# Moving the statistics of a token tile ahead of the apply before it, and one copy from VectorE to ScalarE, in the first loop of an 8-core attention and slot-router layer

## The chip, the cores and the metric

The kernel runs on all 8 cores of one Trainium2 chip, the same program on each, with no exchange between them. The metric is the device time of the slowest core, in microseconds (us), and the median over runs. A core has five engines that work side by side: PE (TensorE, matmuls and transposes), ACT (ScalarE, functions of one input), DVE (VectorE, elementwise work and reductions), POOL (GpSimd) and SP (SyncE); the last two here only issue transfers. Each runs its own instructions in program order and meets the others through semaphores.

## The reference

The input is x of shape (2, 8192, 1024). One layer is `x + s * silu(f)`, with s an attention block with MLP on the normalised x, and f a slot router on the same normalised x. The part that the change touches is the router's first half, which every core computes for all 8192 tokens of its batch entry (16 tiles of 512), since it sums over them:

```python
xn = (x - mean(x)) / sqrt(var(x) + 1e-5)              # per token, over 1024
h = gelu(concat([xn, slot_mean]) @ w1 + b1)           # 512 wide
route_logits = (h @ w2 + b2) / (abs(tau) + 0.1)       # 64 slots
topk_vals, topk_idx = top_k(route_logits, 8)
alpha = one_hot(topk_idx) weighted by softmax(topk_vals)
slot_input = einsum('bts,btd->bsd', alpha, xn)        # sum over tokens
denom = alpha.sum(axis=1) + 1e-8
```

Everything after it (a GRU step on the 64 slots, attention among them, the attention block and the MLP for the core's own 2048 tokens) is not touched.

## The kernel before

The program is a series of blocks; at the end of a block all engines meet. The loop of the change is one block. It runs over tiles mt = 0 to 15 of 512 tokens (`N_MT`), each as four subtiles st of 128 tokens. The first four tiles (`own_f(mt)`) are the core's own tokens; their normalised x is kept in float32 (`XN`) and their transposed alpha in `ALPHAT`. What each engine does for a tile, in its program order:

- SP loads x of tile m into one half of `xld` (8 subtile slots, so two tiles) once the apply of tile m-2 is done.
- DVE, `emit_head(mt)`: waits for the load and, for tiles that are not own, for PE's slot-input sums of tile mt-2 (`t_si(mt - 2)`), which read the buffer `xnb` that the tile is going to overwrite. Then statistics (L508, L510: 8 instructions), aggregation (L514), a wait for ACT's sqrt, reciprocal (L519), and four applies (L528), each subtile signalled by itself.
- DVE, `emit_tail(mt-1)`: top 8 of the logits (L543), the exponentials' bias (L550, L555, signalled as `v_tailA`), the mask (L560), then a wait for ACT's exponentials, their sum (L566), reciprocal, and alpha (L580, `v_tailB`). For own tiles it then waits for PE's transposes of alpha (`t_alphat`) and copies them from `pT0` to `ALPHAT` (L589).
- ACT: sqrt(mt) (L720) after the aggregation, the exponentials of tile mt-1 (L698, L707) after `v_tailA(mt-1)`, for own tiles the bfloat16 copies of x (L734), four evacuations of transposes (L742), four GELUs (L751), and the evacuation of the logits to `LOG` (L760). Sqrt, Exp and Gelu each bring a load of a function table, three in a tile.
- PE: four groups of 8 transposes (L648), each group behind the evacuation of the one before, since there is one buffer `pT0`; the first matmul, 32 instructions in four chunks (L662); the logits (L676, L682); then `emit_si(mt-1)`: the slot-input sums (L612, L614, L617), and for own tiles the transposes of alpha into `pT0` (L624).

The semaphore counts are worked out ahead: `VB`, `TB`, `AB` hold how many signals DVE, PE and ACT have given at the start of each tile, and `v_...`, `t_...`, `a_...` turn them into values to wait for. `finv` (L191) signals behind a drain of its engine. `ST` is a tile of 96 small columns: scratch for the statistics, mean and variance in 16 to 23, deviation in 32 to 35, its reciprocal in 36 to 39.

Of the kernel before, what the change touches and what calls it, by code (L numbers as in the profile page):

```python
# [18 lines left out]
N_MT = 16  # L19
# [57 lines left out]
def build_nc(dbg=False):  # L77
# [51 lines left out]
    with ExitStack() as ex:  # L129
# [128 lines left out]
        with ExitStack() as exW:  # L258
# [6 lines left out]
            with ExitStack() as exA:  # L265
# [174 lines left out]
                v_c = t_c = a_c = 0  # L440
                for m in range(N_MT):
                    VB.append(v_c); TB.append(t_c); AB.append(a_c)
                    v_c += 5 + (0 if m == 0 else
                                2 + (1 if own_f(m - 1) else 0))
                    t_c += 9 + (0 if m == 0 else
                                1 + (1 if own_f(m - 1) else 0))
                    a_c += (1 + (0 if m == 0 else 1)
                            + (4 if own_f(m) else 0) + 9)
                VB.append(v_c); TB.append(t_c); AB.append(a_c)

                v_aggr = lambda m: dv0 + VB[m] + 1
                v_apply = lambda m, st: dv0 + VB[m] + st + 2

                def v_tailA(m):
                    return dv0 + (VB[m + 1] + 6 if m + 1 < N_MT
                                  else VB[N_MT] + 1)

                def v_tailB(m):
                    return dv0 + (VB[m + 1] + 7 if m + 1 < N_MT
                                  else VB[N_MT] + 2)  # L460

                v_alphat = lambda m: dv0 + VB[m + 1] + 8
# [16 lines left out]
                a_log = lambda m: ac0 + AB[m] + aoff(m) + 9  # L479

                def a_exp(m):
                    return ac0 + (AB[m + 1] + 2 if m + 1 < N_MT
                                  else AB[N_MT] + 1)

# [3 lines left out]
                with nc.Block() as blk:  # L488
# [10 lines left out]
                    def _(v):  # L499
                        def emit_head(mt):  # L500
                            own = own_f(mt)
                            v.wait_ge(sx[mt % 2], x_wait(mt))
                            if mt >= 2 and not own:
                                v.wait_ge(spe, t_si(mt - 2))
                            v.drain()
                            SB = (0, 40, 64, 76)
                            for st in range(4):
                                v.bn_stats(ST[:, SB[st]:SB[st] + 6],  # L508
                                           xslot(mt, st)[:, 0:512])
                                v.bn_stats(ST[:, SB[st] + 6:SB[st] + 12],  # L510
                                           xslot(mt, st)[:, 512:1024])
                            v.drain()
                            for st in range(4):
                                i = v.bn_aggr(ST[:, 16 + 2 * st:  # L514
                                                 18 + 2 * st],
                                              ST[:, SB[st]:SB[st] + 12])
                            finv(v, sdv, 'dv')
                            v.wait_ge(sac, a_sqrt(mt))
                            v.reciprocal(ST[:, 36:40], ST[:, 32:36])  # L519
                            v.drain()  # L520
                            for st in range(4):
                                xs = xslot(mt, st)
                                if own:
                                    dstx = XN[:, (mt * 4 + st) * 1024:
                                              (mt * 4 + st + 1) * 1024]
                                else:
                                    dstx = xnbs(mt, st)
                                i = v.tensor_scalar(  # L528
                                    dstx, xs,
                                    ST[:, 16 + 2 * st:17 + 2 * st],  # L530
                                    ST[:, 36 + st:37 + st],
                                    ALU.subtract, ALU.mult)
                                finv(v, sdv, 'dv')

                        def emit_tail(mt):
# [51 lines left out]
                            if own:  # L587
                                v.wait_ge(spe, t_alphat(mt))
                                i = v.tensor_copy(  # L589
                                    ALPHAT[:, mt * 512:(mt + 1) * 512],  # L590
                                    pT0[0:64, 0:512])
                                finv(v, sdv, 'dv')

                        for mt in range(N_MT):
                            emit_head(mt)
                            if mt >= 1:
                                emit_tail(mt - 1)
# [3 lines left out]
                    def _(t):  # L601
# [28 lines left out]
                        for mt in range(N_MT):  # L630
                            own = own_f(mt)
                            par = mt % 2
                            for st in range(4):
# [4 lines left out]
                                if st == 0:  # L638
                                    if mt >= 1:
                                        t.wait_ge(sac, a_evac(mt - 1, 3))  # L640
                                    if mt >= 2 and own_f(mt - 2):
                                        t.wait_ge(sdv, v_alphat(mt - 2))
# [49 lines left out]
                    def _(a):  # L692
# [23 lines left out]
                        for mt in range(N_MT):  # L716
                            own = own_f(mt)
                            par = mt % 2
                            a.wait_ge(sdv, v_aggr(mt))
                            i = a.activation(  # L720
                                ST[:, 32:36],
                                ST[:, 17:25].rearrange(
# [40 lines left out]
                            finv(a, sac, 'ac')  # L763
                        emit_exp(N_MT - 1)
# [1309 lines left out]
```

## Time and profile before

| | us |
|---|---|
| median of 3 runs | 2537.71 |
| lowest and highest run | 2509.82, 2544.93 |
| profiled execution | 2485.47 |
| span of its slowest core (core 4) | 2483.9 |
| span of its shortest core (core 1) | 2446.7 |

A row of the timeline gives start, duration, engine, line and operation, tiles written and read, the count of merged instructions, and in brackets how long the engine had been idle and what ended that. A row of a group of instructions gives the count, the busy time, the mean in ns of one, and the idle time ahead. Busy shares over the whole span are PE 50%, DVE 22%, ACT 20%, POOL 5%, and the 16 DMA queues moved 74 GB/s on the mean.

### The profile page before, as it was taken

Reading aid. Unit: us, or ns where it says so; the run is one execution under the profiler, and the core shown is the slowest. Engines: PE = TensorE matmul, PEld = TensorE weight load, DVE = VectorE, ACT = ScalarE, POOL = GpSimd, SP = SyncE. Lnnn points to the kernel's source line nnn. Section 1 sums busy time; section 2 is a strip of 40 time slices with the busy share of each in tenths; the row PEclk is TensorE's granted clock in tenths of the full one; section 3 lists DMA queues with packets and bytes.
Section 4 is the critical chain, followed back from the end, with each engine's and each line's share of the span. In section 5 each row is a group of like instructions: output and inputs, shape, how many; then the busy total and the mean of one; then the engine's idle time right before and its main releaser. Section 6 shows DMA issues by size and latency. Waiting matters only on the chain. (4 is left out here: it accounts for less than half of the span.)

```text
span 2483.9 us, 18900 instructions; the slowest of 8 cores (2446.7 to 2483.9 us)
## 1 busy us (share of the span) xinstructions
PE 1254.0 (50%) x6308; PEld 577.5 (23%) x6308; DVE 536.2 (22%) x1217; ACT 500.4 (20%) x744; POOL 122.3 (5%) x139
## 2 busy tenths in 40 slices
PE   0234444435352432373654634823068688598696
PEld 0112222222121110131222221311023233243242
DVE  0221323232320021222322323131120220300102
ACT  0244332433330010010110100200041241430521
POOL 1000000000001001000000000002201101001000
PEclk9965756666665555585877866956579789699798
DMA  9210011110006623333151341435945918809346
GB/s 178 63 66 36 34 68 34 68 68 35 34 1 100 122 39 52 54 94 76 54 114 42 87 85 60 94 69 106 140 68 51 138 49 85 153 3 116 85 45 91
DMA packets 341425, 183.65 MB, mean 74 GB/s; under 512 B 305171, under 2 KB 309396, under 8 KB 341332
## 3 DMA queue, kind: packets, MB, share of 16 engines
q0 software_dynamic: 182144, 72.72, 25.7%
q1 hardware_dynamic: 159188, 109.74, 15.7%
q8 instruction: 53, 0.87, 0.1%
q14 instruction: 40, 0.33, 0.0%
HBM read 204.81 MB, written 33.56 MB: 96 GB/s over the span
## 5 line engine op out<-in xcount | busy, mean ns | idle before, releaser
L648 PE MATMUL pT<-cIDb,xnb 128*128 128x128 bf16 x512 | 64.8, 307 | 323.6 <-ACTq L191 179.2
L662 PE MATMUL pM<-xnTs,w1ab 128*128 128x512 bf16 x512 | 153.7, 473 | 23.8 <-ACTq L191 23.8
L1959 PE MATMUL pMa<-h2T,fcwb 128*128 128x512 bf16 x512 | 127.5, 394 | 19.4 <-ACTq L191 19.4
L1896 DVE TENSOR_TENSOR y1t<-pTf,y1t 128x512 f32<-128x512 f32 x32 | 22.1, 692 | 525.8 <-PE pTf L1990 525.8
L648 PEld LDWEIGHTS pT<-cIDb,xnb 128*128 128x128 bf16 x512 | 49.6, 139 | 339.3 <-issue 339.3
L1976 PE MATMUL pPb<-g1F,pjcb 128*128 128x512 bf16 x512 | 121.3, 398 | 11.3 <-DMA pjcb<-pjw 11.3
L1959 PE MATMUL pMb<-h2T,fcwb 128*128 128x512 bf16 x512 | 122.8, 383 | 0.0
L1976 PE MATMUL pPa<-g1F,pjcb 128*128 128x512 bf16 x512 | 114.8, 383 | 9.1 <-ACTq L191 4.5
L1559 ACT ACT_TABLE_LOAD x4 | 5.1, 1283 | 510.7 <-PE pBig L1512 510.7
L1943 PE MATMUL pT0d<-cIDb,h2b 128*128 128x128 bf16 x128 | 16.2, 307 | 161.4 <-DVEq L191 100.0
L508 DVE BATCH_NORM_STATS2 ST<-xld 128x6 f32<-128x512 f32 x64 | 43.6, 682 | 225.0 <-PE pDE L617 222.7
L662 PEld LDWEIGHTS pM<-xnTs,w1ab 128*128 128x128 bf16 x512 | 58.6, 117 | 115.2 <-issue 82.3
L1817 POOL DMA_DIRECT2D pjcb<-pjw x32 | 53.6, 1676 | 614.9 <-PE pPa L1976 476.5
L1396 PE MATMUL pBig<-wob,aoT 128*128 128x512 bf16 x256 | 69.1, 431 | 27.1 <-DVEq L191 27.1
L742 ACT ACTIVATE xnTs<-pT 128x1024 bf16<-128x1024 bf16 x64 | 65.5, 1023 | 64.0 <-PE pT L648 61.5
L1678 PE MATMUL pBig<-FQ2h,FK2h 64*128 64x128 bf16 x256 | 32.0, 301 | 90.6 <-DMA scr_ao<-aog 81.8
L1504 PE MATMUL pBig<-wqb,xhT 128*128 128x512 bf16 x256 | 65.4, 414 | 16.1 <-ACTq L191 16.1
L1722 DVE TENSOR_TENSOR AMK<-pBig,cMSK 128x512 bf16<-128x512 f32 x64 | 44.3, 692 | 133.3 <-PE pBig L1678 103.0
L1959 PEld LDWEIGHTS pMa<-h2T,fcwb 128*128 128x128 bf16 x512 | 50.9, 100 | 84.0 <-issue 27.8
L1976 PEld LDWEIGHTS pPb<-g1F,pjcb 128*128 128x128 bf16 x512 | 51.3, 101 | 76.6 <-issue 24.5
L1976 PEld LDWEIGHTS pPa<-g1F,pjcb 128*128 128x128 bf16 x512 | 49.5, 98 | 71.0 <-issue 15.2
L1959 PEld LDWEIGHTS pMb<-h2T,fcwb 128*128 128x128 bf16 x512 | 50.8, 99 | 63.0 <-issue 4.6
(260 smaller groups left out, 1702.3 us busy)
## 6 DMA issues: line engine op xcount, KB each, us to landing
xld<-x8k SPq DMA_DIRECT2D x64, 512.0 KB, 5.5
pjcb<-pjw POOLq DMA_DIRECT2D x32, 1024.0 KB, 10.9
scr_qk<-tmb SPq DMA_DIRECT2D x16, 512.0 KB, 2.6
y1scr<-XN SPq DMA_DIRECT2D x4, 2048.0 KB, 6.9
fcwb<-fcw POOLq DMA_DIRECT2D x32, 256.0 KB, 20.5
y1t<-y1scr SPq DMA_DIRECT2D x4, 2048.0 KB, 10.8
xre<-x8k SPq DMA_DIRECT2D x16, 512.0 KB, 12.1
out<-xre SPq DMA_DIRECT2D x16, 512.0 KB, 3.3
```

The source lines that it names most:

```text
L508: v.bn_stats(ST[:, SB[st]:SB[st] + 6], xslot(mt, st)[:, 0:512])
L648: i = t.transpose(pT0[:, cc * 128:(cc + 1) * 128], xb[:, cc * 128:(cc + 1) * 128], cIDb[:])
L662: i = t.matmul(dstp[:, 0:512], w1ab[:, cc * 512 + ch * 128: cc * 512 + (ch + 1) * 128], xnTs[:, cc * 512:(cc + 1) * 512], start=(cc == 0), ...
L742: i = a.activation(chunked(xnTs, 8, 512)[:, :, st * 128:(st + 1) * 128], chunked(pT0, 8, 128), AF.Identity)
L1396: i = t.matmul(pBig0[:, nh * 512:(nh + 1) * 512], aoT[:, cc * 128:(cc + 1) * 128], wob[:, cc * 1024 + nh * 512: cc * 1024 + (nh + 1) * 512 ...
L1504: i = t.matmul(pBig0[:, nh * 512:(nh + 1) * 512], xhT[:, cc * 512 + st * 128: cc * 512 + (st + 1) * 128], wqb[:, cc * 1024 + nh * 512: cc ...
L1678: i = t.matmul(pBig0[:, (b % 2) * 512 + gl * 128: (b % 2) * 512 + (gl + 1) * 128], FK2h[0:64, g * 128:(g + 1) * 128], FQ2h[0:64, g * 128:( ...
L1722: i = v.tensor_tensor(AMK[:, (b % 2) * 512:(b % 2 + 1) * 512], pBig0[:, (b % 2) * 512:(b % 2 + 1) * 512], cMSK[:], ALU.mult)
L1817: g.dma_start(out=dstap, in_=srcap).then_inc(spj[slot], 16)
L1896: i = v.tensor_tensor(y1v(mt).rearrange("p (s w) -> p s w", s=4)[:, :, d * 128:(d + 1) * 128], pTf[:, :].rearrange("p (s w) -> p s w", s=4 ...
L1959: i = t.matmul(dstp[:, :], fcwb[:, m * 1024 + cc * 128: m * 1024 + (cc + 1) * 128], h2T[:, cc * 512:(cc + 1) * 512], start=(cc == 0), stop ...
L1976: i = t.matmul(dstp[:, :], pjcb[:, (d % 2) * 4096 + m * 128: (d % 2) * 4096 + (m + 1) * 128], g1F[:, m * 512:(m + 1) * 512], start=(m == 0 ...
```

## The change

DVE no longer does a tile's statistics, sqrt wait and apply in one piece. `emit_head` is split into `emit_stats` and `emit_apply`. DVE starts with the statistics of tile 0; then for each tile it waits for ACT's sqrt of that tile, does the statistics of the next tile, the reciprocal and the apply of this one, and the tail of the one before. The wait for the slot-input sums of tile mt-2 stands ahead of the apply. Mean and variance, deviation and reciprocal get two sets of columns each in `ST`, for even and odd tiles (`P_`, `SD_`, `RD_`). The copy of the transposed alpha moves from DVE to ACT, behind the logits' evacuation of the next tile; PE's wait for it moves along. The rest adjusts the counts. In full:

```diff
--- before.py
+++ after.py
@@ -437,29 +437,34 @@
                 dv0 = C['dv']; pe0 = C['pe']; ac0 = C['ac']; ld_s = C['ld']
                 own_f = lambda m: m < N_MT_OWN
                 VB = []; TB = []; AB = []
-                v_c = t_c = a_c = 0
+                v_c = 1
+                t_c = a_c = 0
                 for m in range(N_MT):
                     VB.append(v_c); TB.append(t_c); AB.append(a_c)
-                    v_c += 5 + (0 if m == 0 else
-                                2 + (1 if own_f(m - 1) else 0))
+                    v_c += ((1 if m + 1 < N_MT else 0) + 4
+                            + (2 if m >= 1 else 0))
                     t_c += 9 + (0 if m == 0 else
                                 1 + (1 if own_f(m - 1) else 0))
                     a_c += (1 + (0 if m == 0 else 1)
-                            + (4 if own_f(m) else 0) + 9)
+                            + (4 if own_f(m) else 0) + 9
+                            + (1 if m >= 1 and own_f(m - 1) else 0))
                 VB.append(v_c); TB.append(t_c); AB.append(a_c)
 
-                v_aggr = lambda m: dv0 + VB[m] + 1
-                v_apply = lambda m, st: dv0 + VB[m] + st + 2
+                v_aggr = lambda m: dv0 + (1 if m == 0
+                                          else VB[m - 1] + 1)
+                v_apply = lambda m, st: (dv0 + VB[m]
+                                         + (1 if m + 1 < N_MT else 0)
+                                         + st + 1)
 
                 def v_tailA(m):
-                    return dv0 + (VB[m + 1] + 6 if m + 1 < N_MT
-                                  else VB[N_MT] + 1)
+                    if m + 1 < N_MT:
+                        return (dv0 + VB[m + 1]
+                                + (1 if m + 2 < N_MT else 0) + 5)
+                    return dv0 + VB[N_MT] + 1
 
                 def v_tailB(m):
-                    return dv0 + (VB[m + 1] + 7 if m + 1 < N_MT
-                                  else VB[N_MT] + 2)
-
-                v_alphat = lambda m: dv0 + VB[m + 1] + 8
+                    return v_tailA(m) + 1
+
                 t_transp = lambda m, st: pe0 + TB[m] + st + 1
                 t_h = lambda m, ch: pe0 + TB[m] + 4 + ch + 1
                 t_logit = lambda m: pe0 + TB[m] + 9
@@ -477,10 +482,15 @@
                 a_evac = lambda m, st: ac0 + AB[m] + aoff(m) + st + 1
                 a_gelu = lambda m, ch: ac0 + AB[m] + aoff(m) + 4 + ch + 1
                 a_log = lambda m: ac0 + AB[m] + aoff(m) + 9
+                a_alphat = lambda m: a_log(m + 1) + 1
 
                 def a_exp(m):
                     return ac0 + (AB[m + 1] + 2 if m + 1 < N_MT
                                   else AB[N_MT] + 1)
+
+                P_ = lambda m: 16 + 8 * (m % 2)
+                SD_ = lambda m: 32 if m % 2 == 0 else 88
+                RD_ = lambda m: 36 if m % 2 == 0 else 92
 
                 def x_wait(mt):
                     return 64 * (mt // 2 + 1)
@@ -497,26 +507,31 @@
 
                     @blk.vector
                     def _(v):
-                        def emit_head(mt):
-                            own = own_f(mt)
+                        SB = (0, 40, 64, 76)
+
+                        def emit_stats(mt):
                             v.wait_ge(sx[mt % 2], x_wait(mt))
-                            if mt >= 2 and not own:
-                                v.wait_ge(spe, t_si(mt - 2))
                             v.drain()
-                            SB = (0, 40, 64, 76)
                             for st in range(4):
                                 v.bn_stats(ST[:, SB[st]:SB[st] + 6],
                                            xslot(mt, st)[:, 0:512])
                                 v.bn_stats(ST[:, SB[st] + 6:SB[st] + 12],
                                            xslot(mt, st)[:, 512:1024])
                             v.drain()
+                            pb = P_(mt)
                             for st in range(4):
-                                i = v.bn_aggr(ST[:, 16 + 2 * st:
-                                                 18 + 2 * st],
+                                i = v.bn_aggr(ST[:, pb + 2 * st:
+                                                 pb + 2 * st + 2],
                                               ST[:, SB[st]:SB[st] + 12])
                             finv(v, sdv, 'dv')
-                            v.wait_ge(sac, a_sqrt(mt))
-                            v.reciprocal(ST[:, 36:40], ST[:, 32:36])
+
+                        def emit_apply(mt):
+                            own = own_f(mt)
+                            rd = RD_(mt); pb = P_(mt)
+                            v.reciprocal(ST[:, rd:rd + 4],
+                                         ST[:, SD_(mt):SD_(mt) + 4])
+                            if mt >= 2 and not own:
+                                v.wait_ge(spe, t_si(mt - 2))
                             v.drain()
                             for st in range(4):
                                 xs = xslot(mt, st)
@@ -527,8 +542,8 @@
                                     dstx = xnbs(mt, st)
                                 i = v.tensor_scalar(
                                     dstx, xs,
-                                    ST[:, 16 + 2 * st:17 + 2 * st],
-                                    ST[:, 36 + st:37 + st],
+                                    ST[:, pb + 2 * st:pb + 2 * st + 1],
+                                    ST[:, rd + st:rd + st + 1],
                                     ALU.subtract, ALU.mult)
                                 finv(v, sdv, 'dv')
 
@@ -584,15 +599,13 @@
                                     JUNK[:, st * 64:(st + 1) * 64],
                                     ALU.mult, ALU.mult)
                             finv(v, sdv, 'dv')
-                            if own:
-                                v.wait_ge(spe, t_alphat(mt))
-                                i = v.tensor_copy(
-                                    ALPHAT[:, mt * 512:(mt + 1) * 512],
-                                    pT0[0:64, 0:512])
-                                finv(v, sdv, 'dv')
-
+
+                        emit_stats(0)
                         for mt in range(N_MT):
-                            emit_head(mt)
+                            v.wait_ge(sac, a_sqrt(mt))
+                            if mt + 1 < N_MT:
+                                emit_stats(mt + 1)
+                            emit_apply(mt)
                             if mt >= 1:
                                 emit_tail(mt - 1)
                         emit_tail(N_MT - 1)
@@ -639,7 +652,8 @@
                                     if mt >= 1:
                                         t.wait_ge(sac, a_evac(mt - 1, 3))
                                     if mt >= 2 and own_f(mt - 2):
-                                        t.wait_ge(sdv, v_alphat(mt - 2))
+                                        t.wait_ge(sac,
+                                                  a_alphat(mt - 2))
                                 else:
                                     t.wait_ge(sac, a_evac(mt, st - 1))
                                 xb = xnbs(mt, st)
@@ -717,9 +731,10 @@
                             own = own_f(mt)
                             par = mt % 2
                             a.wait_ge(sdv, v_aggr(mt))
+                            pb = P_(mt); sd = SD_(mt)
                             i = a.activation(
-                                ST[:, 32:36],
-                                ST[:, 17:25].rearrange(
+                                ST[:, sd:sd + 4],
+                                ST[:, pb + 1:pb + 9].rearrange(
                                     "p (s two) -> p s two",
                                     two=2)[:, :, 0:1].squeeze(2),
                                 AF.Sqrt, bias=SCAL[:, 7:8])
@@ -761,6 +776,12 @@
                                 LOG[:, par * 256:(par + 1) * 256],
                                 pL[:, :], AF.Identity)
                             finv(a, sac, 'ac')
+                            if mt >= 1 and own_f(mt - 1):
+                                a.wait_ge(spe, t_alphat(mt - 1))
+                                i = a.activation(
+                                    ALPHAT[:, (mt - 1) * 512:mt * 512],
+                                    pT0[0:64, 0:512], AF.Identity)
+                                finv(a, sac, 'ac')
                         emit_exp(N_MT - 1)
 
                 assert C['dv'] == dv0 + VB[N_MT] + 2, (C['dv'],
```

## Rows read from the trace of the kernel before

**Rows 1.** Spans of the cores: us from first to last instruction, mean granted clock.

```profile
core 4: 2483.9 us, clock 0.732
```

**Rows 2.** Busy time by stage, core 4: length, busy us of each engine (instructions), clock.

```profile
94.76:750.50 655.74, 289.83 (x1552) 147.40 (x1552) 188.07 (x532) 239.93 (x352) 0.00 (x0) 0.66 0.12 45
```

**Rows 3.** Timeline of one tile, mt = 11, and its neighbours' ends.

```profile
538.38 0.38 ACT L760 ACTIVATE LOG<-pLa 128x256 f32<-128x256 f32 x1 [1.89 <-PE pLa L682]
...
540.33 0.69 DVE L508 BATCH_NORM_STATS2 ST<-xld 128x6 f32<-128x512 f32 x1 [21.07 <-PE pDE L617]
...
545.78 1.28 ACT L720 ACT_TABLE_LOAD   x1 [7.02 <-DVEq L191]
...
547.75 3.62 DVE L528 TENSOR_SCALAR xnb<-xld,ST 128x1024 bf16<-128x1024 f32 x4
...
556.84 1.02 ACT L742 ACTIVATE xnTs<-pT 128x1024 bf16<-128x1024 bf16 x1 [0.15 <-issue]
...
577.12 0.38 ACT L760 ACTIVATE LOG<-pLb 128x256 f32<-128x256 f32 x1 [1.89 <-PE pLb L682]
```

**Rows 4.** Waits of DVE and ACT, 335 to 700 us: total, times, longest.

```profile
DVE ST L508 <- PE pDE L617: 199.5, 9, 22.9
...
ACT L720 <- DVEq L191: 72.9, 9, 8.7
```

**Rows 5.** Timeline of the first two tiles, DVE and ACT.

```profile
102.36 0.18 DVE L519 RECIPROCAL ST<-ST 128x4 f32<-128x4 f32 x1 [1.83 <-ACTq L191]
102.62 3.62 DVE L528 TENSOR_SCALAR XN<-xld,ST 128x1024 f32<-128x1024 f32 x4
...
106.48 0.69 DVE L508 BATCH_NORM_STATS2 ST<-xld 128x6 f32<-128x512 f32 x1 [0.24 <-issue]
...
128.63 0.38 ACT L760 ACTIVATE LOG<-pLa 128x256 f32<-128x256 f32 x1 [1.73 <-PE pLa L682]
129.16 1.28 ACT L720 ACT_TABLE_LOAD   x1
...
130.87 0.18 DVE L519 RECIPROCAL ST<-ST 128x4 f32<-128x4 f32 x1 [19.05 <-ACTq L191]
131.13 3.61 DVE L528 TENSOR_SCALAR XN<-xld,ST 128x1024 f32<-128x1024 f32 x4
```

**Rows 6.** The transposed alpha's copy and its apply (timeline); two ACT evacuations (groups).

```profile
167.99 0.42 DVE L589 COPY ALPHAT<-pT 64x512 bf16<-64x512 bf16 x1 [26.36 <-PE pT L624]
...
176.08 3.62 DVE L528 TENSOR_SCALAR XN<-xld,ST 128x1024 f32<-128x1024 f32 x4
...
L742 ACT ACTIVATE xnTs<-pT 128x1024 bf16<-128x1024 bf16 x64 | 65.5, 1023 | 64.0 <-PE pT L648 61.5 <-issue 2.5
...
L760 ACT ACTIVATE LOG<-pLa 128x256 f32<-128x256 f32 x8 | 3.1, 383 | 15.0 <-PE pLa L682 15.0
```

**Rows 7.** Timeline at the start of the last tile.

```profile
698.62 0.38 ACT L760 ACTIVATE LOG<-pLa 128x256 f32<-128x256 f32 x1 [1.89 <-PE pLa L682]
...
702.21 0.69 DVE L508 BATCH_NORM_STATS2 ST<-xld 128x6 f32<-128x512 f32 x1 [23.17 <-PE pDE L617]
...
707.66 1.28 ACT L720 ACT_TABLE_LOAD   x1 [8.66 <-DVEq L191]
...
709.63 3.62 DVE L528 TENSOR_SCALAR xnb<-xld,ST 128x1024 bf16<-128x1024 f32 x4
```

**Rows 8.** Issue of a load (timeline); stretch behind it: as rows 2, DMA share, GB/s.

```profile
512.50 79.76 SPq L183 DMA_DIRECT2D xld<-x8k  x12
...
521.00:525.00 4.00, 2.02 (x16) 1.55 (x16) 0.00 (x0) 1.45 (x3) 0.00 (x0) 0.50 0.00 0
```

**Rows 9.** First matmul (L662): sum over 16 tiles by stage; timeline of weight load and matmuls.

```profile
sum 638.00, PE 153.69 PEld 58.60; mean PE 9.61 PEld 3.66
...
565.41 0.15 PEld L662 LDWEIGHTS pM<-xnTs,w1ab 128*128 128x128 bf16 x1 [0.27 <-issue]
...
570.84 3.61 PE L662 MATMUL pM<-xnTs,w1ab 128*128 128x512 bf16 x16 [0.31 <-ACTq L191]
```

## The prediction, made before the change was run

> **What bounds the kernel now.** First the spans of the cores: core 4 is the slowest of the profiled execution, 2483.9 us at a mean granted clock of 0.732 [rows 1]; the execution took 2485.5 us, 1.6 us around the span. Then the busy time by stage: the changed loop runs from 94.76 to 750.5 us, 655.7 us, and in it no engine is busy even half of the time (PE 289.8, ACT 239.9, DVE 188.1) [rows 2]. So neither throughput nor transfers bound it, but a chain that goes round the three engines once per tile of 512 tokens; a stage's end counts fully, since the next stage starts at a block boundary.
>
> The timeline of one tile (mt = 11) shows the chain [rows 3]. Logits of tile 10 are evacuated at 538.38. DVE waits for PE's last slot-input sum (pDE, the releaser named in the row at 540.33), since that frees the buffer that the normalised tile will go into, and only then starts the statistics, with the aggregation behind them; ACT loads the sqrt table at 545.78; after sqrt and reciprocal DVE applies the normalisation at 547.75. Then come the top-8 of the tile before, its exponentials on ACT, and only at 556.84 the first evacuation of the transposes, 9 us behind the start of the apply. From there transposes, first matmul, GELU, logits, and the next evacuation at 577.12: 38.74 us for the tile. The two waits that the change works on are read from the table of waits, for starts 6 to 14 (335 to 700 us): DVE's statistics waited 199.5 us for PE in nine times, and ACT sat 72.9 us between a logit evacuation and the sqrt's table load, 8.1 us each [rows 4].
>
> **The change, part by part.** I measure every tile from the start of its predecessor's logit evacuation (LOG) to its first apply. All after the apply (tail, exponentials, evacuations, matmuls) keeps its order, so a gain or loss here shifts the whole rest of the chain.
>
> *Statistics one tile ahead.* The statistics of mt+1 no longer stand before the apply of mt+1, but they stand before the apply of mt: DVE first waits for sqrt(mt), then runs stats(mt+1), then reciprocal and apply(mt). ACT is in program order and does sqrt(mt) behind LOG(mt-1). So the 21 us in which DVE waits are not used: the wait for sqrt(mt) sits in front of stats(mt+1), and the block of 5.45 us (540.33 to 545.78 [rows 3]) remains in the chain, now behind the sqrt. What leaves the chain is (a) the wait for the slot-input sums, which now guards the apply and is long over by then, and (b) the trip to ACT between aggregation and apply, which now starts straight behind LOG.
>
> The new distance: LOG itself 0.38, the gap to the table load 0.15, load to DVE's release 1.71 (129.16 to 130.87). These three stand in the old trace at mt = 1, where the statistics were already done and ACT went straight on [rows 5]. Then the block 5.45, and 0.25 from reciprocal to apply (102.36 plus its duration, apply at 102.62 [rows 5]). Sum 0.38 + 0.15 + 1.71 + 5.45 + 0.25 = 7.94 us. The old distance is 0.38 + the ACT wait + 1.97 (545.78 to 547.75 [rows 3]). The gain of one tile is its ACT wait minus 5.59; over starts 6 to 14 that is 72.9 - 9 x 5.59 = **-22.6 us**. It is 1.4 where PE's sums ran fast (wait 7.02 [rows 3]) and about 3 where they ran at the low clock (wait 8.66 [rows 7]).
>
> *The last tile* has no mt+1. sqrt(15) would be in hand at 698.62 + 2.24 = 700.86; the apply then waits for the sums of tile 13, which released DVE at 702.21; it starts near 702.3 instead of 709.63 [rows 7]: **-7.3 us**.
>
> *The first two tiles lose.* Before, stats(1) ran at 106.48, behind apply(0), while ACT and PE had the tile: free. Now it stands between sqrt(0) and apply(0), which moves from 102.62 by 5.45. At mt = 1 the old apply came directly behind the sqrt (130.87, 131.13 [rows 5]); now stats(2) stands between, again 5.45. Together **+10.9 us**, with nothing that hides them.
>
> *The alpha-transpose copy, DVE to ACT*, for the four own tiles (starts 2 to 5). Before: PE's transposes released the DVE copy at 167.99, and the apply came at 176.08, so 8.09 from release to apply [rows 6]. Now: the copy on ACT. No such row exists; its bounds are the 383 ns for 256 columns and 1023 ns for 1024 columns [rows 6]; on the line through both, 512 columns take about 0.60. Then 0.15, 1.71, 5.45, 0.25: 8.16. So **+0.3 us** for four, and between -0.6 and +2.0 with the two bounds. ACT keeps three table loads per tile, as the copy sits behind another Identity. What queues behind its wait is only the sqrt, counted here. PE's wait moves from DVE to ACT for a thing that either had done long before.
>
> *Double buffering of mean, deviation and reciprocal*: columns of a small tile, no instruction, nothing.
>
> *Transfers.* Each x tile is now read one tile (about 39 us) earlier, while its load is issued behind the same apply as before. The load issued at 512.50 has left the queues by 521: they stand at a share of 0.00 from there to 525 [rows 8]. The statistics that read it would now start near 540 (before, near 579). Margin about 19 us or more, so nothing; if a load did take longer than that it would cost its excess in each tile.
>
> Sum: -22.6 - 7.3 + 10.9 + 0.3 = **-18.7 us**, 2485.5 to 2466.8 us, -0.75%. Bounds of the main term: if PE's sums had all run fast, each gain is 7.02 - 5.59 = 1.43 and the total -9.0; if all slow (8.66 - 5.59 = 3.07), -23.7.
>
> Beside this, one rule of the Trainium skill speaks against the plan. The old trace shows 0.15 us between the end of LOG and the table load, and a load of 1.28 [rows 5]. The Trainium skill (ScalarE: Activation LUTs, "What ACT_TABLE_LOAD costs") counts a drain of about 1.38 us to each switch of set beside the 1283 ns of the load. By it, an estimate, the sqrt right behind LOG would pay 1.38 more than the one that came after a long idle, and starts 6 to 14 would gain about 12 us less: -6 us in all. The trace agrees with the load's length, not with the drain, so my sum does without it.
>
> **The profiled execution and the median.** The runs shown have a median of 2537.7 (2509.8 to 2544.9); the profiled one lies 2.1% under it and under all three. The same 18.7 us off the median give **2519 us**. The ratio is what I trust; the absolute number carries the scatter of the runs, 35 us.
>
> **Rivals.**
> 1. *The statistics are hidden after all*, that is stats(mt+1) runs in DVE's wait and the block leaves the chain in every tile. Price: starts 2 to 14 and the first two no longer pay 5.45, 15 x 5.45 = up to 82 us more, 2385 us on the profiled time (-4%). For it: 20 us of idle DVE in each tile. Against: it needs sqrt(mt) early, and ACT cannot reach it before LOG(mt-1). Chance 0.03.
> 2. *The shorter loop keeps PE's clock up.* PE waits about 1.4 to 3 us less before each tile. The 16 first matmuls of a block often run at the low clock, 0.15 + 0.28 = 0.43 each by their weight loads, the last 16 in 3.61, 0.226 each, and a block takes 9.6 on the mean (153.69 / 16) [rows 9]. At the high level all 32 take 7.2, 2.4 less: 14 x 2.4 = 34 more, so -53 us, 2433 (-2.1%). Against: the idle between sums and transposes only shrinks to 7 us, the transposes still stand apart by the exponentials, and the granted clock there is 0.50 [rows 8]. Chance 0.05. The Trainium skill (TensorE: Matmul & The Clock Gate, "Loop structure matters more than you think") says that closing gaps between matmuls keeps the array at its higher clock; the direction is this rival's.
> 3. *Slower: the matmul block falls wholly into the low clock.* The clock rises inside the block today. If the new period puts the rise behind it, 32 x 0.43 = 13.8 instead of 9.6, +4.2 a tile. It decides from about +1.2 us per tile on (18.7 / 15); in full +62 - 19 = +43, 2529 on the profiled time (+1.7%), 2581 on the median's. For it: a block today already holds matmuls of both kinds, so the place of the rise is open. Against: the mean of 16 blocks is 9.6 [rows 9], far from 13.8, and less idle ahead of a block is no reason for a later rise. Chance 0.05.
> 4. *Nothing measurable comes through*, since the clock's rise shifts by what is gained: 2485 and 2538. It takes part of the -9 bound with it. Chance 0.12.
>
> The forecast has 0.75. Comparisons of this kernel can tell about 2%. The forecast and rival 4 are within it; rival 1 and 2 mostly beyond it as faster, and scatter may carry -0.75% past -2% once in thirty: faster 0.09, same 0.87, slower 0.04 (rival 3 mostly stays below 2%, scatter carries it over). The range takes the bounds (-24 to 0), part of rivals 2 and 3, and the scatter of the runs: 2480 to 2550.
>
> **What would show it.** In the new trace a tile in the middle: LOG, table load 0.15 behind it, statistics released by ACT (not by PE's sums) 2.24 after LOG, apply 7.9 after LOG. Periods around 37.3 to 37.9 instead of 38.7 to 41. Apply(0) and apply(1) each 5.45 later in their tile; ACT's copy about 0.60. The loop near 637 us, all stages behind it unchanged. I am wrong if statistics start before LOG ends, if the first-matmul block's mean leaves 9.6 by more than 1 us, or if DVE waits for a load.

## The result and the profile after

| | before | changed |
|---|---|---|
| median of the first comparison | 2490.92 us (25 runs) | 2473.89 us (24 runs) |
| ratio, 95% interval | | 0.9929 [0.9908, 0.9950] |
| median of the repetition | 2475.56 us (12 runs) | 2454.45 us (8 runs) |
| ratio, 95% interval | | 0.9905 [0.9868, 0.9942] |
| span of the slowest core, profiled | 2483.9 us (core 4) | 2469.9 us (core 3) |

The change makes the kernel 0.7% faster, less than the 2% that one comparison can tell, but clear of 1 in both intervals. Some executions of this program, before and changed alike, show a lower clock on one die and take 1 to 6% more; the ratios leave them out, the medians do not.

The page of the changed kernel, its span and the group of the statistics (count, then busy us and mean ns, then the idle time ahead and its releaser):

```profile
span 2469.9 us, 18900 instructions; the slowest of 8 cores (2431.9 to 2469.9 us)
...
L516 DVE BATCH_NORM_STATS2 ST<-xld 128x6 f32<-128x512 f32 x64 | 43.6, 681 | 327.6 <-ACTq L191 327.1
```

The statistics last what they did and DVE still idles ahead of them, now for ACT. The table of waits for starts 6 to 14 (330 to 660 us: total, times, longest) says the same as a pair, and answers to [rows 4]:

```profile
DVE ST L516 <- ACTq L191: 192.0, 9, 21.9
```

```profile
ACT L712 <- DVEq L191: 100.0, 9, 11.5
```

The same wait, in front of the exponentials, in the kernel before (335 to 700 us):

```profile
ACT L698 <- DVEq L191: 49.2, 9, 5.6
```

DVE waited 199.5 us for PE's sums and now 192.0 for ACT's sqrt. ACT's wait in front of the sqrt (72.9) is gone from the table; instead it waits 11.1 us a tile in front of the exponentials, where before it waited 5.5. The stall changed its place and shrank: ACT's two waits took 8.1 + 5.5 = 13.6 us a tile, the one that is left takes 11.1. The timeline of one tile (mt = 11, core 3), against [rows 3]:

```profile
533.42 0.38 ACT L775 ACTIVATE LOG<-pLa 128x256 f32<-128x256 f32 x1 [1.89 <-PE pLa L696]
...
533.94 1.28 ACT L735 ACT_TABLE_LOAD   x1
...
535.04 0.17 PE L630 MATMUL pDE<-cCOL,alsc 128*64 128x1 bf16 x1
535.24 0.30 ACT L735 ACTIVATE ST<-ST,SCAL 128x4 f32<-128x4 f32 x1
535.78 0.69 DVE L516 BATCH_NORM_STATS2 ST<-xld 128x6 f32<-128x512 f32 x1 [21.32 <-ACTq L191]
...
541.23 0.18 DVE L531 RECIPROCAL ST<-ST 128x4 f32<-128x4 f32 x1
541.49 3.62 DVE L543 TENSOR_SCALAR xnb<-xld,ST 128x1024 bf16<-128x1024 f32 x4
...
570.95 0.38 ACT L775 ACTIVATE LOG<-pLb 128x256 f32<-128x256 f32 x1 [1.89 <-PE pLb L696]
```

From the evacuation of the logits to the apply it is 541.49 - 533.42 = 8.07 us (before 9.37 in this tile and 11.01 where the sums were slow), and the tile takes 37.53 us, where before it took 38.7 to 41. The statistics are still inside that distance.

The loop runs from the first statistics to the first instruction of the block behind it. On core 3 of the changed kernel:

```profile
94.28 0.69 DVE L516 BATCH_NORM_STATS2 ST<-xld 128x6 f32<-128x512 f32 x1 [0.54 <-PEq L408]
...
727.15 0.15 DVE L797 TENSOR_SCALAR ST<-pDE 64x1 f32<-64x1 f32 x1 [4.26 <-PEq L498]
```

that is 632.9 us. Read in this way on all eight cores, and with what remains of each core's span behind it:

| kernel | loop, mean of 8 cores (range) | the rest, mean (range) |
|---|---|---|
| before | 652.9 (647.0 to 659.1) | 1723.8 (1702.4 to 1734.1) |
| changed | 633.1 (631.8 to 634.7) | 1726.1 (1705.8 to 1742.8) |
| changed, repetition | 633.5 (632.3 to 634.6) | 1718.1 (1707.7 to 1726.1) |

The loop lost 19.8 us. The rest scatters by 32 and 37 us between the cores of one execution without any change of code; that is why the two spans on the page differ by 14 us and not by 20.

### The profile page after: what moved, and what is told of

Same layout as the page of the kernel before. It is cut to its first block and busy times, and to the rows that moved or that the text cites. A ratio compares the mean times of both kernels' runs of the same rounds, so it can differ in the third digit from the quotient of the medians.

```text
span 2469.9 us, 18900 instructions; the slowest of 8 cores (2431.9 to 2469.9 us)
## 1 busy us (share of the span) xinstructions
PE 1239.4 (50%) x6308; PEld 571.3 (23%) x6308; DVE 533.6 (22%) x1213; ACT 503.1 (20%) x748; POOL 122.3 (5%) x139
## 5 line engine op out<-in xcount | busy, mean ns | idle before, releaser
L662 PE MATMUL pT<-cIDb,xnb 128*128 128x128 bf16 x512 | 64.4, 306 | 315.0 <-ACTq L191 229.2
L676 PE MATMUL pM<-xnTs,w1ab 128*128 128x512 bf16 x512 | 150.0, 463 | 24.2 <-ACTq L191 24.2
L1997 PE MATMUL pPa<-g1F,pjcb 128*128 128x512 bf16 x512 | 120.9, 397 | 17.3 <-DMA pjcb<-pjw 12.8
L662 PEld LDWEIGHTS pT<-cIDb,xnb 128*128 128x128 bf16 x512 | 49.3, 138 | 329.5 <-issue 329.5
L1997 PE MATMUL pPb<-g1F,pjcb 128*128 128x512 bf16 x512 | 113.1, 379 | 4.1 <-DMA pjcb<-pjw 4.1
L676 PEld LDWEIGHTS pM<-xnTs,w1ab 128*128 128x128 bf16 x512 | 56.7, 114 | 113.9 <-issue 80.9
L1819 POOL DMA_DIRECT2D fcwb<-fcw x32 | 28.1, 927 | 747.4 <-DMA y1scr<-XN 709.8
## 6 DMA issues: line engine op xcount, KB each, us to landing
pjcb<-pjw POOLq DMA_DIRECT2D x32, 1024.0 KB, 10.9
y1t<-y1scr SPq DMA_DIRECT2D x4, 2048.0 KB, 11.4
```

Source lines behind the costliest of these rows:

```text
L662: i = t.transpose(pT0[:, cc * 128:(cc + 1) * 128], xb[:, cc * 128:(cc + 1) * 128], cIDb[:])
L676: i = t.matmul(dstp[:, 0:512], w1ab[:, cc * 512 + ch * 128: cc * 512 + (ch + 1) * 128], xnTs[:, cc * 512:(cc + 1) * 512], start=(cc == 0), ...
L1997: i = t.matmul(dstp[:, :], pjcb[:, (d % 2) * 4096 + m * 128: (d % 2) * 4096 + (m + 1) * 128], g1F[:, m * 512:(m + 1) * 512], start=(m == 0 ...
```

## The experiments

The theory: one chain goes round the engines once per tile, and only what leaves the chain shortens it. Each experiment is a variant of one of the two kernels; its loop is measured as above.

**Statistics ahead of the sqrt wait.** The changed kernel with two statements exchanged.

```diff
-                            v.wait_ge(sac, a_sqrt(mt))
                             if mt + 1 < N_MT:
                                 emit_stats(mt + 1)
+                            v.wait_ge(sac, a_sqrt(mt))
                             emit_apply(mt)
```

> The changed kernel with two statements exchanged: the statistics of tile mt+1 come ahead of the wait for sqrt(mt), not behind it. Theory 1 (the wait for the sqrt is what keeps the statistics in the chain): the distance from the logits' evacuation to the apply falls from 8.1 to about 2.5 us (or 3.6, where the slot-input sums run at the low clock); tiles 2 to 5 gain 5.4 each, 6 to 14 gain 4.5 to 5.5, tile 15 nothing, tile 1 gains 5.4, tile 0 1.8. Together 70 to 78 us: the loop falls from 633 to 555-563 us, the ratio to the kernel before is about 0.962-0.966. Theory 2 (the statistics are already off the chain, and what was gained came from somewhere else): no change against the changed kernel, ratio 0.993. Theory 3 (the shorter loop moves the rise of PE's clock to an unlucky place): the distance falls as in theory 1, but the first-matmul blocks take over 11 us instead of 9.4, and half of the gain or less arrives.

Measured: ratio to the kernel before 0.9593 [0.9567, 0.9619]; loop 559.0 us (553.3 to 564.0), 74.1 less than the changed kernel. The timeline of one tile (core 1):

```profile
489.20 0.70 DVE L516 BATCH_NORM_STATS2 ST<-xld 128x6 f32<-128x512 f32 x1 [0.70 <-DMA xld<-x8k]
...
507.69 0.39 ACT L775 ACTIVATE LOG<-pLb 128x256 f32<-128x256 f32 x1 [1.89 <-PE pLb L696]
...
509.93 0.18 DVE L531 RECIPROCAL ST<-ST 128x4 f32<-128x4 f32 x1 [15.38 <-ACTq L191]
...
511.31 3.62 DVE L543 TENSOR_SCALAR xnb<-xld,ST 128x1024 bf16<-128x1024 f32 x4 [1.21 <-PE pDE L630]
```

The statistics run at 489, while PE has the matmul block still ahead, and the apply follows the logits by 3.62 us, held at the end by the slot-input sums at the low clock (granted clock 0.56 between 507.69 and 511.31). The loop lies in the 555 to 563 that theory 1 gave; the ratio is 0.003 to 0.007 below what was written, since here the rest is 11 us shorter on the mean than before, without a change of its code (1712.6 against 1723.8). Theory 2 falls. The load of x is now late for the statistics (0.70 us), but DVE idles 15.4 us behind them, so it costs nothing. The matmul blocks of this kernel take 147.4 us in all against 150.0 in the changed one, so theory 3 finds nothing here.

**The wait for the sums alone.** The kernel before with one statement moved, nothing else.

```diff
                             v.wait_ge(sx[mt % 2], x_wait(mt))
-                            if mt >= 2 and not own:
-                                v.wait_ge(spe, t_si(mt - 2))
                             v.drain()
...
                             v.reciprocal(ST[:, 36:40], ST[:, 32:36])
+                            if mt >= 2 and not own:
+                                v.wait_ge(spe, t_si(mt - 2))
                             v.drain()
```

> The kernel before with one statement moved: the wait for the slot-input sums of tile mt-2 goes from ahead of the statistics to ahead of the apply. No double buffering, copy of alpha still on DVE. Theory 1: DVE does the statistics in its idle time for tiles 6 to 15, their distance falls from about 10.4 to 2.5-3.6, about 7 to 8 us each; tiles 0 to 5 as before (there the copy of the transposed alpha holds DVE). 70 to 80 us less, the loop near 577 us, ratio 0.968-0.972. So this single statement would bring about four times what the whole change brings. Theory 2: no more than the wait for the sums itself, about 1.5 to 3 us in ten tiles, ratio 0.99.

Measured: 0.9748 [0.9689, 0.9806]; loop 577.7 us (573.7 to 579.2), 75.2 less than before. The loop came out as theory 1 had it (577); the ratio is 0.003 to 0.007 above what was written. It comes from four runs, of which one took 2432.1 us and the others 2398.0 to 2404.5; the medians alone (2404.3 and 2472.9) give 0.972. One statement, with no double buffering, brings almost four times what the whole change does (75.2 against 19.8).

**The wait for the sums put back.** The changed kernel, with it ahead of the statistics.

```diff
                             v.wait_ge(sac, a_sqrt(mt))
+                            if mt >= 2 and not own_f(mt):
+                                v.wait_ge(spe, t_si(mt - 2))
                             if mt + 1 < N_MT:
                                 emit_stats(mt + 1)
```

> The changed kernel with the wait for the slot-input sums put back ahead of the statistics (behind the sqrt wait). It separates the two waits that the change took out. Theory 1 (the gain is the sqrt's trip, which now runs beside the sums; the wait for the sums is over at about the same time): the sums end about 2.0 us behind the evacuation at the high clock, the sqrt 2.4, so nothing at the high clock and 1.2 us a tile at the low one: 0 to 12 us slower than the changed kernel, ratio to before 0.993-0.998. Theory 2 (the gain is the wait for the sums): all of the gain of tiles 6 to 14 is given back, about 20 us, ratio 1.00.

Measured: 0.9948 [0.9915, 0.9982]; loop 635.7 us, 2.6 more than the changed kernel: six cores at 632.4 to 635.2, two at 641.1 and 641.3. Those two are cores 2 and 3. What they take more lies mostly in starts 2 to 5 (175.6 and 175.7 us, the others 169.2 to 171.6), and there their granted clock differs; the four us behind the start of LOG at start 3, on core 2 and on core 0 (columns as in [rows 2], the granted clock third from the end):

```profile
223.30:227.30 4.00, 2.47 (x16) 1.27 (x14) 0.00 (x0) 1.67 (x3) 0.00 (x0) 0.81 0.00 0
```

```profile
219.60:223.60 4.00, 2.03 (x16) 1.12 (x14) 0.00 (x0) 2.10 (x3) 0.00 (x0) 1.00 0.00 0
```

At starts 2 and 3 the wait that was put back is not even executed, so it is not what held these two cores. The other six have 633.8 on the mean, 0.7 more than the changed kernel. So of the two waits that the change took off the chain, the one for the sums was worth little by itself here; the sqrt's trip, which now runs beside the sums, is where the gain comes from. Theory 2 wanted 20 us back.

This holds for sums at the high clock. At starts 6 to 14 of the eight cores, 72 in all, the sums were slow (PE busy for over 3 of the four us behind the start of LOG, where 1.8 is fast) twice in this run, and 41 times in the kernel before. At the two slow ones (start 6 of cores 2 and 3) the distance from logits to apply is 9.41 us, where the changed kernel has 8.08 and the kernel before 11.0. So with slow sums the two waits have a share each, 1.3 us for the sums and 1.6 for the sqrt's trip; this rests on two tiles.

**The copy of the transposed alpha back on DVE.** The changed kernel, with these lines at the end of the tail and the counts adjusted; ACT's copy is out.

```diff
                             finv(v, sdv, 'dv')
+                            if own:
+                                v.wait_ge(spe, t_alphat(mt))
+                                i = v.tensor_copy(
+                                    ALPHAT[:, mt * 512:(mt + 1) * 512],
+                                    pT0[0:64, 0:512])
+                                finv(v, sdv, 'dv')
```

> The changed kernel with the copy of the transposed alpha back on DVE, at the end of the tail of the four own tiles. Theory 1: the sqrt of tiles 2 to 5 no longer waits for PE's transposes, so it runs beside them, DVE's copy ends about 0.6 us behind the transposes and the statistics follow at once: the distance of tiles 2 to 5 falls from 10.5 to about 8.6 (2.3 to the transposes, 0.66 for the copy, 5.45, 0.25), that is 4 x 1.9 = 7 us faster, ratio to before 0.990. Theory 2 (moving the copy to ACT is part of the gain): slower than the changed kernel, ratio 0.995 or more.

Measured: 0.9876 [0.9855, 0.9896], a little below the 0.990 that was written; loop 625.2 us, 7.9 less than the changed kernel, where 7 was written. The changed kernel's start of tile 2 (core 3):

```profile
175.87 0.38 ACT L775 ACTIVATE LOG<-pLb 128x256 f32<-128x256 f32 x1 [1.73 <-PE pLb L696]
178.07 0.59 ACT L781 ACTIVATE ALPHAT<-pT 64x512 bf16<-64x512 bf16 x1 [1.81 <-PE pT L637]
178.80 1.28 ACT L735 ACT_TABLE_LOAD   x1
...
186.35 3.61 DVE L543 TENSOR_SCALAR XN<-xld,ST 128x1024 f32<-128x1024 f32 x4
```

and the same with the copy on DVE (core 3):

```profile
172.88 0.39 ACT L780 ACTIVATE LOG<-pLb 128x256 f32<-128x256 f32 x1 [1.73 <-PE pLb L701]
...
173.41 1.28 ACT L740 ACT_TABLE_LOAD   x1
...
175.08 0.42 DVE L604 COPY ALPHAT<-pT 64x512 bf16<-64x512 bf16 x1 [25.77 <-PE pT L643]
175.81 0.69 DVE L516 BATCH_NORM_STATS2 ST<-xld 128x6 f32<-128x512 f32 x1 [0.31 <-issue]
...
181.53 3.62 DVE L543 TENSOR_SCALAR XN<-xld,ST 128x1024 f32<-128x1024 f32 x4
```

10.48 us from logits to apply against 8.65. On ACT the copy's wait for PE's transposes holds up the sqrt queued behind it; on DVE the same wait lies beside the sqrt, whose table load starts at 173.41, 0.14 behind LOG. This part of the change works against the other.

**The first two tiles in the old order.** The changed kernel, with the statistics of tiles 1 and 2 behind apply and tail.

```diff
-                            if mt + 1 < N_MT:
+                            if mt + 1 < N_MT and not late(mt):
                                 emit_stats(mt + 1)
                             emit_apply(mt)
                             if mt >= 1:
                                 emit_tail(mt - 1)
+                            if late(mt):
+                                emit_stats(mt + 1)
```

> The changed kernel, but at tiles 0 and 1 the statistics of the next tile come behind the apply and the tail, as in the kernel before; from tile 2 on as changed. Theory 1 (these two statistics blocks were free before and are paid in the changed kernel): 10.9 us less than the changed kernel, the loop 622 against 633, ratio to before 0.9885. Theory 2 (DVE has slack there too): no difference, 0.993.

Measured: 0.9867 [0.9813, 0.9921]; loop 622.1 us, 11.0 less than the changed kernel's 633.1 and 11.4 less than its repetition. Expected was 10.9.

**The changed kernel once more.**

> The changed kernel once more, unaltered, on another occasion. If the ratio is the property of the change and the absolute time that of the occasion, the ratio comes out within 0.990 to 0.996 again, while both absolute medians may lie 10 to 20 us from those of the first comparison (2474 and 2491). If the absolute time were the steadier of the two, this one would come out at 2474 within 5 us whatever the kernel before does.

Measured: 0.9905 [0.9868, 0.9942], with medians of 2454.5 and 2475.6 us. The ratio agrees with the first one within its interval; the changed kernel's own time came out 19 us lower than the first time, the kernel before 15 lower. On a third occasion the kernel before had 2472.9 (13 runs). The absolute time belongs to the occasion, the ratio to the change; it would have taken 2474 within 5 us for the other reading. What differs between the occasions, the chip or something else, was not tested.

**A version that beats both.** Order on DVE: statistics of mt without any wait but the load; top 8, bias and mask of tile mt-1; the waits; apply of mt; the rest of the tail. The tail is split in two, the counts adjusted, the alpha copy on DVE between the two halves.

```diff
                         for mt in range(N_MT):
-                            v.wait_ge(sac, a_sqrt(mt))
-                            if mt + 1 < N_MT:
-                                emit_stats(mt + 1)
+                            emit_stats(mt)
+                            if mt >= 1:
+                                emit_tailA(mt - 1)
+                            if cp_f(mt):
+                                v.wait_ge(spe, t_alphat(mt - 2))
+                                i = v.tensor_copy(
+                                    ALPHAT[:, (mt - 2) * 512:
+                                           (mt - 1) * 512],
+                                    pT0[0:64, 0:512])
+                                finv(v, sdv, 'dv')
+                            v.wait_ge(sac, a_sqrt(mt))
                             emit_apply(mt)
                             if mt >= 1:
-                                emit_tail(mt - 1)
+                                emit_tailB(mt - 1)
```

> A candidate that should beat both: order on DVE is statistics of mt (in its idle time, no wait but the load), top 8 and bias of tile mt-1, for own tiles the copy of the transposed alpha, the waits for sqrt and sums, apply of mt, rest of the tail of mt-1. ACT can then do the exponentials straight behind the sqrt, beside the apply. Theory 1 (one chain round the engines; what leaves it shortens every tile): from the evacuation of the logits to the first evacuation of transposes 6.3 us instead of 18.5 before (0.38 + 0.15 + 1.58 + 0.1 + 1.28 + 2.67), and 20.3 from there on, 26.6 us a tile where before had 40.2; own tiles 4.8 more for ACT's copies; the loop about 460 us, ratio about 0.92. Theory 3 (PE's clock or the loads take part of it back): the load of x then has only about 15 us, and the matmul blocks may run at the low clock for longer; if the blocks go from 9.4 to 13.7 the loop is about 520, ratio 0.945.

Measured: 0.9197 [0.9142, 0.9252], a median of 2293.6 us against 2475.6 on the same occasion; loop 459.7 us (458.8 to 460.7). The timeline of one tile (core 5):

```profile
411.05 0.38 ACT L784 ACTIVATE LOG<-pLa 128x256 f32<-128x256 f32 x1 [1.89 <-PE pLa L705]
...
411.57 1.28 ACT L744 ACT_TABLE_LOAD   x1
411.61 0.61 DVE L556 MAX8 TKS<-LOG 128x8 f32<-128x64 f32 x4 [13.88 <-ACTq L191]
...
413.31 1.28 ACT L721 ACT_TABLE_LOAD   x1
...
414.66 3.61 DVE L542 TENSOR_SCALAR xnb<-xld,ST 128x1024 bf16<-128x1024 f32 x4 [1.02 <-PE pDE L640]
...
417.32 1.02 ACT L766 ACTIVATE xnTs<-pT 128x1024 bf16<-128x1024 bf16 x1 [0.15 <-issue]
```

The first transposes are evacuated 6.27 us behind the logits, not 18.5, since the exponentials no longer wait for the apply. The expectation had 6.3; its terms add up to 6.16. This was not in the prediction's view: with the statistics hidden, the order apply, top 8, exponentials was the next dear piece of the chain, and larger than the statistics. Starts 6 to 14, which hold neither copies of alpha nor first tiles, take 338.3 us on the mean of eight cores in the changed kernel, 292.9 with the statistics hidden and 240.1 here: 45.4 us for the statistics, 52.8 for the split tail. The matmul blocks take 149.3 us in all, against 150.0 in the changed kernel, so theory 3 finds nothing here either.

## Where the prediction was right and where it was wrong

**The mechanism** held. The statistics stay in the chain behind the wait for the sqrt; the exchange of two statements shows it (74.1 us).

**The sum** was -18.7 us. The loop lost 19.8 on the mean of eight cores, but the sum was made from rows of core 4, and there the loop went from 655.8 to 632.2, 23.6 less. That the sum meets the mean so well is in part luck: core 4's loop was 2.9 us above the mean before, and one term had the wrong sign. Cut at the start of LOG, core 4 before and changed:

```profile
165.79 0.38 ACT L760 ACTIVATE LOG<-pLb 128x256 f32<-128x256 f32 x1 [1.73 <-PE pLb L682]
...
336.88 0.38 ACT L760 ACTIVATE LOG<-pLb 128x256 f32<-128x256 f32 x1 [1.89 <-PE pLb L682]
```

```profile
174.84 0.38 ACT L775 ACTIVATE LOG<-pLb 128x256 f32<-128x256 f32 x1 [1.73 <-PE pLb L696]
...
344.04 0.38 ACT L775 ACTIVATE LOG<-pLb 128x256 f32<-128x256 f32 x1 [1.89 <-PE pLb L696]
...
682.43 0.38 ACT L775 ACTIVATE LOG<-pLa 128x256 f32<-128x256 f32 x1 [1.89 <-PE pLa L696]
```

| core 4, us | before | changed | difference | forecast |
|---|---|---|---|---|
| first two tiles | 71.0 | 81.3 | +10.3 | +10.9 |
| starts 2 to 5 | 171.1 | 169.2 | -1.9 | +0.3 |
| starts 6 to 14 | 361.7 | 338.4 | -23.4 | -22.6 |
| last tile | 52.0 | 43.3 | -8.7 | -7.3 |

By its terms:

- The distance from logits to apply was put at 7.94 and is 8.07. The missing 0.13 lies between sqrt and statistics: 0.24 from the end of the sqrt (535.54) to 535.78, where the reciprocal in [rows 5] had come after 0.12.
- Starts 6 to 14: 22.6 forecast on core 4's waits. With 8.07 it would be 21.4, and the nine distances from logits to apply did lose 21.4 (94.1 to 72.7). The other 1.9 of the 23.4 lies elsewhere in the tiles. The tile of 37.5 us lies in the 37.3 to 37.9 forecast.
- Last tile: the apply follows the logits by 2.49 us. It was said to wait for the sums until about 3.7; here (core 3) the sums ran at the high clock, a granted clock of 1.00 from LOG to the apply, and the sqrt came last:

```profile
683.85 0.39 ACT L775 ACTIVATE LOG<-pLa 128x256 f32<-128x256 f32 x1 [1.89 <-PE pLa L696]
...
686.34 3.62 DVE L543 TENSOR_SCALAR xnb<-xld,ST 128x1024 bf16<-128x1024 f32 x4
```

- The first two tiles: +10.9 forecast, 11.0 and 11.4 by the experiment. In the trace the old order of [rows 5] is gone:

```profile
102.00 0.69 DVE L516 BATCH_NORM_STATS2 ST<-xld 128x6 f32<-128x512 f32 x1 [1.96 <-ACTq L191]
...
107.46 0.18 DVE L531 RECIPROCAL ST<-ST 128x4 f32<-128x4 f32 x1
107.72 3.62 DVE L543 TENSOR_SCALAR XN<-xld,ST 128x1024 f32<-128x1024 f32 x4
```

- The copy on ACT: 0.60 forecast, 0.59 measured, and 8.28 from PE's release to the apply where 8.16 was forecast. What failed in this term is that one tile's 8.09 stood for all four of the kernel before: on core 4 its distances from logits to apply were 10.29, 12.33, 10.31 and 10.53, now 10.48, 10.43, 10.42 and 10.42. At the 12.33 (start 3) the granted clock in the four us behind LOG was 0.59, at starts 2 and 4 it was 1.00. So +0.3 came out as -1.7. What the prediction also did not see is that with the copy left on DVE the sqrt would have run beside the transposes: the placement costs 7.9 us against leaving the copy where it was.

**The absolute time** was wrong. 2519 us was forecast with 2480 to 2550; the median is 2473.9, 6 us below the range. The step that failed is the one on the profiled execution and the median. Its working had the sum on the profiled execution, 2466.8, and then carried the 18.7 us over to a median of three runs, 2537.7. That median was not the kernel's: the three are the first of the 25 runs, whose median is 2490.9, and of the other 22 only two took more than 2500. Why the first came out high stays open, as no clocks were kept for them. The profiled execution (2485.5), 2.1% below their median and below all three, was the better witness. The sum itself was close, as the changed kernel's profiled execution took 2471.4. Carried to 2490.9 the same ratio gives 2472; the measured ratio is 0.9929, the forecast one 0.9925. The lower end of the range was set from the three runs' scatter, though the text itself had a value of 2467 in hand.

**The rivals.** Rival 1 (statistics hidden) was no property of this change, but its price was about right: 74.1 us in the first experiment where 82 at most was written. Rivals 2 and 3 (the clock) did not occur: the matmul blocks took 9.38 us on the mean of 16, before 9.61 [rows 9], and neither 7.2 nor 13.8. Rival 4 (nothing comes through) did not occur either: both intervals of the ratio stay below 1. The changed kernel's sum over the 16 stages, for L676 alone:

```profile
sum 613.00, PE 150.04 PEld 56.66; mean PE 9.38 PEld 3.54
```

**The drain.** The load follows the evacuation's end by 0.14 us (533.80 to 533.94) and lasts 1.28. In none of the 15 tiles behind the first is the gap between the ACTIVATE ahead and the sqrt's load more than 0.15, and the sum that did without a drain is the one that held. The Trainium skill (ScalarE: Activation LUTs, "What ACT_TABLE_LOAD costs") would have the sqrt behind the evacuation pay a drain of 1.38 us beside the load; the trace agrees with its load and not with its drain.

## What to carry to other kernels

Moving work ahead in program order helps only when the wait in front of it moves too: ask what the engine's last wait before the moved piece is, and whether that is released earlier. A wait belongs directly in front of the first instruction that needs it; here one statement in the right place was worth 75 us and a restructuring around it 20. And a forecast in absolute time wants a check of its baseline: when the profiled execution and a median of three differ by 2%, the range must reach to both. And a term that is taken from one tile and multiplied wants a look at the other tiles first: one of four was 2 us longer.

## What the runs showed of the hardware beyond that

The loop's length scatters over 12 us between the cores before (647.0 to 659.1) and over 3 in the changed kernel (631.8 to 634.7). Before, the sums of PE stood in the chain and took 2.0 or 3.6 us by the granted clock at that moment. The four us behind the start of LOG at starts 6 and 11, core 4 before; the same 12 matmuls keep PE busy for 3.45 or 1.77 us:

```profile
336.90:340.90 4.00, 3.45 (x12) 1.40 (x10) 0.39 (x1) 0.37 (x1) 0.00 (x0) 0.59 0.00 0
538.40:542.40 4.00, 1.77 (x12) 0.86 (x10) 2.07 (x4) 0.36 (x1) 0.00 (x0) 1.00 0.00 0
```

Of nine starts (6 to 14) three are slow on core 5 and eight on cores 0 and 7. The nine distances from logits to apply add up to 89.2 us on core 5 and 97.6 on cores 0 and 7, and the stretch takes 355.2 and 365.3: most of the 12 us. In the changed kernel the distances add up to 72.7 on every core and the stretch takes 337.9 to 338.6.

Two things changed at once. The sums are off the chain: at start 6 they are still slow on four cores, and the distance is 8.08 there too. And they are fast at 67 of the 72 starts, where before they were at 31. What keeps the clock up at that moment stays open; the run with the wait put back has it too (70 of 72), the run with the statistics ahead of the sqrt wait has slow sums again, and its cores scatter over 11 us. The run with the split tail has them too, but as many on each core (its nine distances add up to 27.7 or 27.8), and scatters over 2.
